# Three DRAM copies of FFN weights, issued by ScalarE on its own queue, earlier in the program, instead of by SyncE

## The reference, cut to what matters

```
k = x @ Wk.T ; v = x @ Wv.T ; k = rotary(k)
for each block of 16 positions (4096 / 16 = 256 of them, in order):
    z = k_c @ W                        # per batch and head, 16x32 @ 32x32
    W = W - k_c.T @ ((z - v_c) * 2 / (16 * 32))
x = layernorm(x + layernorm(z)*gamma+beta @ Wo.T)
x = layernorm(x + (silu(x @ gate_w.T * gate_s) * (x @ up_w.T * up_s)) @ down_w.T * down_s)
```

## Time and profile before

| | |
|---|---|
| median of 3 runs | 2058.8 us (2057.78 to 2060.44) |
| the profiled execution | 2054.83 us, of which the span 2052.7 us |
| PE busy | 1949.6 us, 95% of the span |
| DVE / ACT / POOL busy | 1219.4 / 938.1 / 582.4 us |
| granted clock, mean | 0.977 |
| DMA queue q1 | 210768 packets, 173.08 MB, 28.2% of 16 engines' span |

### The profile page before, as it was taken

The page is one execution under the profiler, slowest core; times in us unless marked ns, Lnnn a source line. Parts: engine busy times, 40 slices in busy tenths (PEclk is TensorE's granted clock), DMA queues, the critical chain, the costliest instruction groups (busy, mean ns, idle before and its releaser), DMA issues.

```text
span 2052.7 us, 54706 instructions
## 1 busy us (share of the span) xinstructions
PE 1949.6 (95%) x22424; PEld 1550.6 (76%) x22424; DVE 1219.4 (59%) x2814; ACT 938.1 (46%) x2258; POOL 582.4 (28%) x651
## 2 busy tenths in 40 slices
PE   5669999999999999999999999999999999998887
PEld 3347877778787777878777787877778787777775
DVE  3484665666566566656656665665666566565532
ACT  2324444444444444445444444544444454444421
POOL 2012323223332322333232233323323332332332
PEclk9769999999999999999999999999999999999999
DMA  6842222222332222232222223222222322222110
GB/s 208 265 132 82 86 88 60 82 73 86 94 88 86 61 82 71 87 95 85 89 60 83 67 90 94 87 87 59 85 73 84 94 88 86 63 82 56 49 35 21
DMA packets 211019, 176.61 MB, mean 86 GB/s; under 512 B 34193, under 2 KB 165521, under 8 KB 210577
## 3 DMA queue, kind: packets, MB, share of 16 engines
q1 hardware_dynamic: 210768, 173.08, 28.2%
HBM read 105.86 MB, written 75.76 MB: 88 GB/s over the span
## 4 chain that ended last, share of the span: by engine, by line
PE 90%; DVE 5%; ACT 2%; issue 1%; SPq 1%; DMA 1%; POOL 0%; POOLq 0%; DVEq 0%
PE gu_acc L616 35%; PE work L597 28%; PE down_acc L628 14%; PE state_acc L587 5%; PE z_acc L570 4%; PE work L604 3%; PE gu_acc L604 1%; DVE err L799 1%; DVE fm L828 1%; ACT fm L475 1%; SPq L286 1%; DVE low_half L864 1%; DVE hid L806 1%; ACT hid L451 1%; DMA v_rows<-v_scr 0%
## 5 line engine op out<-in xcount | busy, mean ns | idle before, releaser
L799 DVE TENSOR_TENSOR err<-z_acc,v_rows 32x256 f32<-32x256 f32 x1024 | 430.0, 420 | 177.8 <-PE z_acc L570 148.9
L378 POOL TENSOR_TENSOR hid_lo<-hid,hid_hi 128x256 fp32r<-128x256 f32 x352 | 267.2, 759 | 912.0 <-ACT hid_hi L461 911.9
L427 ACT ACTIVATE state<-state_acc 32x256 f32<-32x256 f32 x1028 | 385.5, 375 | 87.9 <-PE state_acc L587 63.9
L616 PE MATMUL gu_acc<-x_hi,gw 128*128 128x256 f32 x1408 | 385.8, 307 | 8.6 <-DVE x_lo L843 3.6
L616 PE MATMUL gu_acc<-x_hi,uw 128*128 128x256 f32 x1408 | 349.7, 281 | 0.0
L616 PE MATMUL gu_acc<-x_lo,gw 128*128 128x256 f32 x1408 | 349.6, 281 | 0.0
L616 PE MATMUL gu_acc<-x_lo,uw 128*128 128x256 f32 x1408 | 349.3, 281 | 0.0
L806 DVE SCALAR_TENSOR_TENSOR hid<-gu_acc,up_scale,hid 128x256 f32<-128x256 f32 x352 | 170.2, 484 | 297.3 <-ACT hid L451 296.4
L440 ACT ACTIVATE v_rows<-z_acc 128x256 f32<-128x256 f32 x256 | 98.6, 385 | 521.3 <-DVE err L799 521.3
L616 PEld LDWEIGHTS gu_acc<-x_hi,gw 128*128 128x128 f32 x1408 | 266.0, 189 | 59.8 <-DVE hid L806 23.8
L628 PE MATMUL down_acc<-dw,hid_hi 128*128 128x512 f32 x704 | 284.2, 404 | 2.8 <-POOL hid_lo L378 2.8
(11 more groups left out here) (67 smaller groups left out, 2117.3 us busy)
## 6 DMA issues: line engine op xcount, KB each, us to landing
x_fm<-xT SPq DMA_DIRECT2D x64, 256.0 KB, 3.3
k_scr<-k_tok SPq DMA_DIRECT2D x32, 512.0 KB, 2.9
k_rows<-k_scr SPq DMA_DIRECT2D x512, 32.0 KB, 1.9
v_rows<-v_scr SPq DMA_DIRECT2D x512, 32.0 KB, 1.8
z_scr<-v_rows SPq DMA_DIRECT2D x512, 32.0 KB, 1.7
z_tok<-z_scr SPq DMA_DIRECT2D x32, 512.0 KB, 3.9
x_tok<-x SPq DMA_DIRECT2D x32, 512.0 KB, 3.5
out<-x_tok SPq DMA_DIRECT2D x32, 512.0 KB, 2.9
```

Of the source, the lines that this page charges most:

```text
L378: pool.tensor_tensor(hid_lo[m % RING][:], hid[m % 2][:], hid_hi[m % RING][:].bitcast(F32), ALU.subtract).then_inc(hid_lo_ready, 1)
L427: act.activation(state[q, :, e].rearrange("p (r g) e -> p r g e", r=2), state_acc[q, :, 0:P].rearrange("p r (g e) -> p r g e", e=HEAD), AC ...
L616: mm = pe.matmul(gu_acc[:, k * TOK:(k + 1) * TOK], lhsT=w[:, c, m * P:(m + 1) * P].bitcast(dt), rhs=part[:, c].bitcast(dt), start=(c == 0 ...
L799: dve.tensor_tensor(err[q, g:g + 2, :, :].rearrange("p a (r h) e -> p a r (h e)", r=2), z_acc[q, :, 0:P].rearrange("p r (a c) -> p a r c", ...
```

## The change

SP no longer issues the three copies. ScalarE issues them instead, as three DMAs in its own program, on its own DMA queue, right behind the high part of Wv in slot 12 of tick -1. The semaphore and who waits for it stay as they are.

```diff
@@ SP, tick @@
                 if t.within():
                     load_rows(t.par, 0, k_sent[0], v_sent[0])
 
-                if t.reg is None and t.off == 0:
-                    for dst, src in ((gw_scr, gwT), (uw_scr, uwT), (dw_scr, dwT)):
-                        sp.dma_start(dst, src).then_inc(ffn_copied, 16)
                 if t.reg is None and t.off == 1:
                     load_ffn(1)
@@ ScalarE, tick @@
                         act.wait_ge(wv_in, 16 * NC)
                         for c in range(NC):
                             high_part(wv, (x_tok, z_tok), c)
+                        for dst, src in ((gw_scr, gwT), (uw_scr, uwT), (dw_scr, dwT)):
+                            act.dma_start(dst, src).then_inc(ffn_copied, 16)
```

## The result

The changed kernel takes 2070.33 us (median of 4 runs, 2069.49 to 2070.83) against 2058.77 before (4 runs): ratio 1.0057, 95% interval 1.0043 to 1.0071. It is 11.6 us slower. The forecast was 2073.9 with a range of 2060 to 2078.

A forecast was written before the change was run, and what follows sets the result against it. TensorE bounds the kernel from 163 us on, a chain of single results the filling before. x 15.5 us later less 0.4 relief gives +15.1 on 2054.83, 2069.9; plus 4.0 to the median, 2073.9, range 2060 to 2078.

The forecast's parts named there:

- The term that counted: Copies moved earlier, from 14.23 to 43.4 us, beside SP's small transfers: tile 1's x arrives 15.5 us later.
- the upper bound: Tile 1's x gets through only when the copies are over, at 47.6 us; chance 0.52, 2070 to 2078.
- the 8 or 9: Turns of one small SP piece per 45 KB packet, 2.2 us each, between 24.79 and 43.4 us; V's pieces use them up.
- The relief: Second half of tile 0's scan: err no longer waits for V's rows behind the copies, gain 0.4 us.
- the 0.83 taken from the first step: Usual distance of err behind z, 0.60 us plus 0.23 for longer matmuls, putting the fifth err at 72.62.
- next in line is the scan itself: Why the relief is no more than 0.4 us: z at 71.79 waited 1.85 us for the state.
- ScalarE's issues: Three DMA issues added to ScalarE, 1.8 us from 14.23, covered by its idle time until 20.25: cost 0.
- their slack: Tile 0's rows land by 56.5, the scan's first err comes at 63.3: 7 us to spare.
- the 2 to 3 us set aside: Allowance either way in the main case's range for the clock's slow stretches falling otherwise.
- turns of several pieces: Rival: an engine takes about 16 SP pieces per turn, x lands by 42; middle +8 us, 2064 to 2069, chance 0.22.
- Shared bytes: Rival: K's store and x get half of the engines beside the copies; +3.8 us less 0.4, 2062, chance 0.12.
- Let through: Rival: SP's small transfers need not wait for 45 KB packets, x lands at 32 to 33; 2054 to 2059, chance 0.14.

The follow-up runs named there:

- e3: Changed kernel with only the gate and up copies issued early by ScalarE, the third by SP at its old place: 2061.58 us, ratio to before 1.0016.
- e10: Changed kernel with only the gate copy issued early by ScalarE, the other two by SP at their old place: 2056.55 us, ratio to before 0.9997.
- e5: Changed kernel with tile 1's x and its rotary table loaded ahead, issued by SP behind Wo's loads: 2066.53 us, ratio to before 1.004.
- e8: Kernel before with the bias matmuls moved from tick 1 into PE's idle gaps of tick 0: 2058.03 us, ratio 1.0001.
- e4: Control: the kernel before with one more blank line, for a second profile of it: 2057.54 us, ratio 0.9997, span 2056.3.
- e7: e5 with ScalarE waiting until tile 1's x is in SBUF before it issues the three copies: 2068.64 us, ratio to before 1.0053.
- e1: Kernel before with the three copies issued early on SP's own queue, right behind Wo's loads: 2070.28 us, ratio 1.0056.
- e2: Kernel before with the three copies on ScalarE's queue but late, after the first half of tile 0's rows: 2057.32 us, ratio 0.9999.

## Why the prediction was right

**The term that counted.** "I take the upper bound": x gets through when the copies are over. Right, by three observations: x's 17.1 us to landing, the dose (e3, e10), and e5's x that was issued at once and landed at the end. The reading of the packets was right in the main: 60 against 60 and 17 against 17, and V's pieces do fill the time, landing 0.2 us behind the last copy. But SP got fewer turns than the 8 or 9 counted from 24.79 on: q1's first packets ran only between 28 and 29 us, and by 38 us 79 had gone, about 5 for an engine. Why the first turn came over 4 us behind the issue is open.

**Its size.** Predicted 15.5 us later, measured 13.05. The main piece that failed is the copies' start, put at "14.23 (13.09 + 1.14)". It was 11.46: the issue waited for Wv's arrival, as the activations did, and not for these to end. 2.2 us of the difference are that, the other 0.6 are Wv's arrival, which was sooner in this execution (11.44 against 12.03). 11.46 + 29.2 would have given 40.7, and x at 44.9; it was 45.1, but by two errors that cancel. The copies took 30.7 us from the first issue to the last landing and not 29.2: their first packets ran between 14 and 15 us, and until then q1 kept the engines busy with the end of Wo's loads, which the prediction had left out. And x came 3.0 us behind the copies and not 4.2.

**The relief.** Predicted 0.4 us, measured 0. The fifth err no longer waits for V's rows, but starts no sooner behind its z:

```profile
85.51 1.78 DVE L798 TENSOR_TENSOR err<-z_acc,v_rows 32x256 f32<-32x256 f32 x4 [1.59 <-PE z_acc L569]
```

That is 1.23 us behind z at 84.28, as in the kernel before (71.79 to 73.02), and the 0.83 taken from the first step was too short for the fifth. The rows landed just when the step could begin anyway. The shift from the projection to the fifth z shrinks by 0.56 all the same, since matmuls ran at a higher clock: 0.36 us in tile 1's projection of K (5.13 us at clock 0.55, against 5.49 at 0.50) and 0.4 in the bias matmuls (4.66 at 0.77, against 5.04 at 0.71), less 0.2 lost between them. And the reason given, "next in line is the scan itself", left out that the bias matmuls had hidden most of what the rows cost, as e8 showed.

**The rest.** ScalarE's issues cost 0, as said. Tile 0's rows kept their slack: issued to 50.9, first err at 60.5. From the fifth z to the first FFN matmul the shift shrank by another 0.5 us (12.49 to 11.95). On the way it was down to 10.8, at the projection of K at 106.70, and grew again as matmuls of the changed kernel ran slower (Wo's projection 4.63 us against 4.37); that lay within the 2 to 3 us set aside. On top stood the 4.0 us from profile to median, which were added to the span's sum and belonged to a quick execution (e4); since only the difference counts, no harm came of it. In all 15.1 predicted, 11.6 measured. The number alone would not have told the cause: it lies 1.3 us above the 2069 at which the range of "turns of several pieces" ends. The rows do.

**The rivals.** Turns of several pieces is refuted: a turn takes one small packet. The rule named with it from the Trainium skill, page "DMA: Bandwidth & Descriptors", section "Queues, rings and completion order", that engines go round between queues by whole packets, agrees with the trace in its first half (60 and 60, 17 and 17, in e5 118 and 121 packets); the 9 to 17 descriptors that it calls typical for one packet, and so for one turn, do not show here: SP's 60 packets moved 0.12 MB, 2 KB each, one for each packet on the other queue. Shared bytes: 0.12 against 1.98 MB. Let through: x would have landed at 32.

## What to carry to other kernels

A bulk copy costs by what waits while it runs, not by the queue it is on or the engine that issues it: place it in a stretch in which nothing with a deadline is sent, and cut it so that it ends there. Beside packets of 45 KB a transfer of small ones hardly moves, even when it is issued ahead of two of the three copies (e5); and stores out of a buffer that is soon reused are as urgent as loads. When an edit on the chain gains nothing, look for a second wait that ends at the same time: here two edits that gained 0 each (e8, e10) gained 4.2 us together.

## What the runs showed that I had not expected

- ScalarE's DMAs were issued at 11.46, up to 1.6 us before the activations in front of them in the program had started (the last at 13.02), and 2.2 before these had ended. Where a copy should begin behind other work on that engine, a semaphore has to say so (e7: 17.73).
- A small DMA can hold SP back: beside the copies SP stood 11.80 us at one of 32 KB, once V's and K's stores and x were waiting, and in e5 12.26 us at V's store behind x.
- Three copies on either queue end at nearly the same distance from the last issue: 29.4 us from ScalarE and 29.0 from SP when early (e1), 27.9 from either when late (e2 and the kernel before).
